# Product-key mixing: the second and third piece of the weight multiplied on GpSimd instead of the vector engine

## The reference, cut to what matters

```python
def _L0_ffn_ref(x, w_q, keys, expert_down, expert_up, norm_w):
    H, DK, K = (8, 128, 8)
    NKEYS = 64                      # 64 * 64 = 4096 experts
    xn = _rmsnorm(x, norm_w)
    q = (xn @ w_q.T).reshape(b, t, H, 2, DK)
    sim1 = jnp.einsum('bthd,hkd->bthk', q[..., 0, :], keys[:, :, 0, :])
    sim2 = jnp.einsum('bthd,hkd->bthk', q[..., 1, :], keys[:, :, 1, :])
    s1, i1 = jax.lax.top_k(sim1, K)
    s2, i2 = jax.lax.top_k(sim2, K)
    all_idx = (i1[..., :, None] * NKEYS + i2[..., None, :]).reshape(b, t, H, K * K)
    all_sc = (s1[..., :, None] + s2[..., None, :]).reshape(b, t, H, K * K)
    fs, pk = jax.lax.top_k(all_sc, K)
    fi = jnp.take_along_axis(all_idx, pk, axis=-1)
    hidden = jax.nn.gelu(jnp.einsum('btd,bthkd->bthk', xn, expert_down[fi]), approximate=False)
    hidden = hidden * jax.nn.relu(fs)
    return jnp.einsum('bthk,bthkd->btd', hidden, expert_up[fi])
```

## Time and profile before

| What | us |
|---|---|
| median of 3 runs | 523.21 |
| lowest, highest | 519.38, 525.88 |
| the profiled execution's own time | 523.5 |
| its span, first to last instruction | 521.7 |
| TensorE busy in the span | 465.3 |
| vector engine busy | 286.6 |
| scalar engine busy | 171.2 |
| GpSimd busy | 4.1 |
| the mixing stage, from its first matmul to its last weighing | 318.9 to 350.0 |

### The profile page before, as it was taken

The page is one execution under the profiler, slowest core; times in us unless marked ns, Lnnn a source line. Parts: engine busy times, 40 slices in busy tenths (PEclk is TensorE's granted clock), DMA queues, the critical chain, the costliest instruction groups (busy, mean ns, idle before and its releaser), DMA issues.

```text
span 521.7 us, 8539 instructions
## 1 busy us (share of the span) xinstructions
PE 465.3 (89%) x3199; PEld 325.7 (62%) x3199; DVE 286.6 (55%) x925; ACT 171.2 (33%) x428; POOL 4.1 (1%) x6
## 2 busy tenths in 40 slices
PE   3888999878999889977769989989979999889997
PEld 2534554443545459874456878878855668767774
DVE  5155777455767644457746997960045444445332
ACT  1154555434555511364731232000013233124110
POOL 0000000000000000000000002000000000000000
PEclk9898999889999999998888999659999999989999
DMA  8300001000002910800004945600048000000000
GB/s 293 105 2 1 1 0 42 1 0 0 0 0 61 363 64 1 322 2 1 1 1 142 336 143 188 136 0 0 1 132 318 1 1 0 1 0 2 0 1 21
DMA packets 21469, 35.02 MB, mean 67 GB/s; under 512 B 1663, under 2 KB 18048, under 8 KB 20864
## 3 DMA queue, kind: packets, MB, share of 16 engines
q1 hardware_dynamic: 21440, 34.64, 20.5%
HBM read 34.37 MB, written 0.26 MB: 66 GB/s over the span
## 4 chain that ended last, share of the span: by engine, by line
PE 73%; DVE 16%; issue 5%; ACT 2%; DMA 1%; DVEq 0%; SPq 0%; POOL 0%; ACTq 0%
PE bank L553 6%; PE bank L538 6%; PE bank L793 6%; PE bank L931 5%; PE bank L527 4%; PE bank L495 4%; PE bank L847 3%; PE bank L492 3%; PE bank L493 3%; PE bank L825 3%; PE bank L826 3%; PE bank L783 2%; PE bank L471 2%; PE bank L945 1%; DMA region_a<-in_Wq 1%
## 5 line engine op out<-in xcount | busy, mean ns | idle before, releaser
L1002 ACT ACTIVATE region_g<-bank,nm_new 128x512 f32<-128x512 f32 x64 | 43.4, 683 | 59.8 <-DVE nm_new L1250 59.8
L538 PEld LDWEIGHTS bank<-ident,region_g 128*128 128x128 f32 x256 | 28.8, 145 | 36.3 <-ACT region_d L1014 24.4
L538 PE MATMUL bank<-ident,region_g 128*128 128x128 f32 x256 | 36.9, 289 | 12.1 <-ACT region_d L1014 7.4
L1245 DVE CUSTOM_DVE_ANT_0 bank<-bank,bias_h 128x512 f32<-128x512 f32 x64 | 43.0, 713 | 4.5 <-issue 4.5
L527 PE MATMUL bank<-region_a,qT 64*128 64x512 f32 x128 | 34.6, 619 | 0.0
L1221 DVE COPY region_a<-bank 128x512 f32<-128x512 f32 x18 | 12.5, 692 | 38.3 <-PE bank L497 38.3
L553 PE MATMUL bank<-region_d,region_a 128*64 128x256 f32 x256 | 32.8, 400 | 0.0
L793 PE MATMUL bank<-region_u,region_g 128*128 128x256 f32 x128 | 29.6, 396 | 1.5 <-issue 1.5
L318 ACT ACTIVATE root<-var 128x2 f32<-128x2 f32 x6 | 1.2, 203 | 87.7 <-DVE var L328 87.7
L783 PE MATMUL bank<-region_a 64*128 64x32 bf16 x768 | 27.3, 249 | 2.4 <-DVE region_a L1499 1.8
L793 PEld LDWEIGHTS bank<-region_u,region_g 128*128 128x128 f32 x128 | 25.5, 200 | 5.3 <-issue 1.6
(11 more groups left out here) (299 smaller groups left out, 833.9 us busy)
## 6 DMA issues: line engine op xcount, KB each, us to landing
region_d<-in_downT SPq DMA_DIRECT2D x2, 2048.0 KB, 10.6
region_u<-in_up SPq DMA_DIRECT2D x2, 2048.0 KB, 11.9
region_a<-in_ctx SPq DMA_DIRECT2D x1, 3072.0 KB, 16.5
region_d<-in_w_q SPq DMA_DIRECT2D x1, 2048.0 KB, 12.3
region_d<-in_ctxT SPq DMA_DIRECT2D x1, 2048.0 KB, 11.5
region_u<-in_wg SPq DMA_DIRECT2D x1, 1728.0 KB, 7.8
region_u<-in_wu SPq DMA_DIRECT2D x1, 1728.0 KB, 11.7
region_a<-in_wd SPq DMA_DIRECT2D x1, 1664.0 KB, 15.9
```

What stands on the lines that cost most here:

```text
L538: mm = nc.tensor.transpose(bank[4 + e][:, k * P:(k + 1) * P], prob[:, u % 2, e, k * P:(k + 1) * P], ident[:, :])
L1002: nc.scalar.activation(prob[:, u % 2, e, :], bank[2 * s + e][:, :], ACT.Exp, scale=-1.0, bias=nm_new[:, p, t, e:e + 1], accum_out=l_blk[:, ...
L1245: ins = nc.vector.tensor_tensor_reduce(bank[2 * s + e][:, :], bank[2 * s + e][:, :], bias_h[:, t, :], -1.0, 3e38, ALU.add, ALU.min, accum_ ...
```

## The change

GpSimd makes the products for the pieces w = 1 and w = 2; the vector engine keeps w = 0. A new semaphore `rest_ready` counts GpSimd's part, and TensorE waits for it beside `hot_ready`. GpSimd's two multiplications of a step wait for that step's `hit_ready`; they stand behind the memset and a wait for its end.

```diff
@@ -290,6 +290,7 @@
+        rest_ready = sem("rest_ready")
@@ -775,6 +776,7 @@
                 for g in range(2):
                     pe.wait_ge(hot_ready, two + (g + 1))
+                    pe.wait_ge(rest_ready, two + (g + 1))
                     pe.wait_ge(hidden_ready, two + (g + 1))
@@ -1495,9 +1497,7 @@
                 nc.vector.tensor_tensor(hit_hi[:, g], iota_h[:, 0:ET], over(1, ET), ALU.is_equal).then_inc(hit_ready, 1)
                 nc.vector.tensor_tensor(hot_lo[:, g], iota_h, over(0, P), ALU.is_equal)
                 dve.wait_ge(hit_ready, n)
-                for w in range(3):
-                    ins = nc.vector.tensor_tensor(hot_hi[:, g, w], hit_hi[:, g], over(2 + w, ET), ALU.mult)
-                ins.then_inc(hot_ready, 1)
+                nc.vector.tensor_tensor(hot_hi[:, g, 0], hit_hi[:, g], over(2, ET), ALU.mult).then_inc(hot_ready, 1)
@@ -1691,6 +1691,20 @@
             pool.wait_ge(down_psum, ET // 2)
             nc.gpsimd.memset(ctxT_b[CD - P:CD - P + 1], 1.0).then_inc(ones4_set, 1)
+            pool.wait_ge(ones4_set, 1)
+
+            def rest_pieces(g, n, at):
+
+                pool.wait_ge(hit_ready, n)
+                for w in (1, 2):
+                    rest = chosen_h[:, 2 + w, bass.ds(at, GS)].unsqueeze(1).to_broadcast([P, ET, GS])
+                    ins = nc.gpsimd.tensor_tensor(hot_hi[:, g, w], hit_hi[:, g], rest, ALU.mult)
+                ins.then_inc(rest_ready, 1)
+
+            with pool.Fori(0, P // GS // 2) as i:
+                two, at = pool.snap(i * 2), pool.snap(i * (2 * GS))
+                rest_pieces(0, two + 1, at)
+                rest_pieces(1, two + 2, at + GS)
```

## The result

| | before | changed |
|---|---|---|
| median of 6 runs, us | 523.33 | 541.82 |
| lowest, highest | 519.38, 525.88 | 539.77, 548.86 |
| the profiled execution's own time | 523.5 | 541.67 |
| its span | 521.7 | 539.9 |

Ratio 1.0389, 95% interval 1.0339 to 1.0439: slower by 17.7 to 23.0 us (the two medians differ by 18.5). The slowest execution of the changed kernel, 548.86 us, showed a lower granted clock than the others, and the ratio leaves it out. The prediction was 534.0 (527 to 542) on a 523.5 base: right in sign, and nearly half of the loss is missing from it. That 541.82 lies just inside the range is luck: the range reached so far only because a multiplication might take 1.7 us, and none takes that by itself. The forecast was +10.5, the ratio says +20, and most of the difference is a term that the prediction did not have.

The account below looks back on a forecast made before the run. TensorE bounds the whole program, the vector engine sets the mixing steps' pace. Later start and GpSimd's chain end step 7 at 359.2 instead of 348.7: 523.5 + 10.5 = 534.0 us, range 527 to 542.

Parts of the forecast that it names:

- The start: Ahead of step 0: TensorE waits for GpSimd's memset and two multiplications, until 324.35 instead of 318.92, costing 5.4 us.
- The loop: Mixing steps: waiting for GpSimd's products makes them 4.52 us each instead of 3.72, with step 7 ending at 359.2.
- The ring: Even and odd steps each form a cycle: chain of 5.6 us plus matmuls of 3.44, 9.05 us per two steps.
- The link that was too dear: End of the loop's chain: after the low one-hot, the vector engine's product, 0.33 us, then GpSimd's two, 2.4 us.
- The signs that I had named: Expected profile: first matmul near 324.3, TensorE idle about 1.1 us a step, GpSimd as releaser, steps about 4.5 us apart.
- Turns, not overlap: In the loop, vector engine and GpSimd instructions reading two SBUF operands alternate, GpSimd behind; chain 5.6 us, chance 0.45.
- rival 1: In the loop, the engines do not hold each other up: chain 4.25 us, +5.6, 529.1 us; chance 0.23.
- The duration of 1.2 us: One GpSimd multiplication in the loop, taken between bounds of 0.45 and 1.7 us, so 2.4 us a step.
- rival 2: GpSimd's multiplication is dear, 1.7 us or more: start 325.35, chain 6.6, +16.2, 539.7 us; chance 0.22.
- rival 3: GpSimd's multiplication is cheap, 0.45 us without turns, TensorE bounds the loop: +1.7, 525.2 us; chance 0.10.
- My ceiling: Most that faster products can win in the mixing steps: 0.28 us in each of eight, 2.2 us, 0.4% of the run.
- The floor of 3.44 us: Time of a mixing step's 96 matmuls on TensorE, below which a step was taken not to fall.

Follow-up runs that it names:

- The two shadow runs: Kernel before, GpSimd's multiplication loaded early, GpSimd also making two unused products a step (534.45 us), or two memsets in their place (521.64 us).
- The version beside the weighing: Changed kernel with only the third piece on GpSimd, run during the vector engine's weighing; tiny multiplication early, memset behind the loop: 518.06 us.
- the control: Kernel before with only the vector engine's loop written out, constants instead of registers: 522.47 us, ratio 0.9988.
- both pieces beside the weighing: Changed kernel with high one-hot ahead of weighing and GpSimd's two products started when matmuls end; tiny multiplication early, memset behind the loop: 523.75 us.
- the run with the memset last: Changed kernel with a tiny GpSimd multiplication issued early and the memset of line 1693 moved behind the loop: 525.14 us, ratio 1.0128.
- the load-alone run: Kernel before plus a tiny GpSimd memset and multiplication behind line 1693's memset, which TensorE awaits ahead of step 0: 535.43 us.
- the last version: Changed kernel, only third piece on GpSimd during the weighing, tiny multiplication early, memset behind the loop, 4 MB of late loads held back: 517.44 us.

## Why the prediction was wrong, point by point

**The start: right in what it counted, and one term missing.** The step that failed is the sum "321.75 + about 0.1 to notice + 2.4 + 0.1 = 324.35", a wait of 5.4 us. With the load out of the way the wait for step 0 is 5.50, so memset and two products were priced well (alone a product lasts 1.14 to 1.17 us: four take 4.52). But between the memset and the first multiplication there were 12.61 us, not 0.1. I took GpSimd's first use of an operation to cost what later ones do. The trace of before could not price it: its only GpSimd instruction besides memsets is the reduction, and the MODIFY_POOL_CONFIG records of its line stand at the very start, at 0.8 us, 228 us ahead of it. But they are there, and I did not ask what they were for. The Trainium skill (GPSIMD Engine Reference, Instruction dispatch) says that the first call to freshly loaded GpSimd code pays about 6 us, 5.95 measured, with no instruction in the profile that shows it. The runs agree in kind and give more: 6.8 to 7.6 us with quiet DMA engines, 10.78 and 12.61 with 4 MB of transfers running. A rival "the code has to be loaded first" belonged into the prediction.

**The loop: right in mechanism, a little too dear.** From step 0 to the last matmul I had 359.2 - 324.35 = 34.85, it was 33.59, against 29.76 before: +3.8 where I counted +5.1. The ring is there: in the changed kernel step 2 ends at 345.33 and step 4 starts at 350.67, 5.34 us for my 5.6; steps come in alternate gaps (4.00, 4.72, 4.06), two of them 8.71 to 8.78 for my 9.05. The link that was too dear is the last: from the low one-hot's end (348.16, where the next instruction starts) to GpSimd's last result (350.56) three products, the vector engine's one and GpSimd's two, took 2.40 us, where I had added up 0.33 + 2.4. The record of GpSimd's first product starts 0.36 us after the low one-hot has started, but it is longer than alone, 1.89 us against 1.15, and ends at 349.27, one product's length behind the one-hot: it waited for it. The vector engine's product then waits behind GpSimd's first, 1.40 us instead of 0.42, which is not the order that I had assumed.

**The signs that I had named.** The first matmul came at 333.26, not near 324.3. The idle time before each later step alternates between 0.6 and 1.3 us, 0.9 in the mean for my 1.1, and the steps are 4.3 us apart in the mean for my 4.5. GpSimd was to stand there as the releaser; the profile names none, but the times above do. "Stretched vector instructions" came true for the product alone; the one-hots kept 0.42 and 1.22 us.

**Turns, not overlap: right.** It was my choice, with no row of before behind it. The two shadow runs show it (3.01 against 1.09 us, and 1.09 when GpSimd only writes), and rival 1 falls. For the second half the rows of before had more than I used: not only the high one-hot but also the low one (1.22) and the three products (1.09) ran under the memset with their usual lengths.

**The duration of 1.2 us: right, with some luck.** It was the middle between bounds of 0.45 and 1.7 that had little behind them. Measured: 1.15 alone, 1.34 in the median over the whole loop, where some wait for their turn. Rivals 2 and 3 fall. The figure of the Trainium skill (GPSIMD Engine Reference, Performance versus the Vector engine), which is for an addition of float32 values, had given an estimate of 1.12 us, close to the 1.15. Two sums of the rivals were wrong without touching the forecast: by its own steps rival 2 ends at 364.2 (539.0 us), not 364.9, and rival 3's chain is 2.75 us, not 2.35.

**The sum.** By stretch: start 5.6 (5.4 expected), loop 3.8 (5.1 expected), load 12.2 (not expected), together 21.6 for 10.5. Without the missing term the forecast would have been a little too high.

**What removing vector work could win: right, but not in this order.** The version beside the weighing took 1.55 us off the stretch, and 3.0 with the pause in step 1 gone as well. My ceiling, "8 x 0.28 = 2.2 us", is met by the 2.3 that are left without the pause, but by two errors that cancel. The floor of 3.44 us for a step is too high, since a lone burst contains the whole last matmul: two steps in one piece take 6.63 us, 3.3 each. And not all eight steps of before waited: the first three ran without a wait, but for the pause. The change itself gave its saving back, since each GpSimd product blocks the vector engine's for about a microsecond (3.01 - 1.09 = 1.92 us for two).

## What to carry to other kernels

The first multiplication on GpSimd carried a cost that no duration shows, in all likelihood a code load (7 us here, over 12 beside bulk transfers): issue a tiny one early, where nobody waits, before judging an offload. When work moves to GpSimd, add up all instructions of both engines that read two SBUF operands as if one engine ran them, and place GpSimd's beside vector instructions that read PSUM. And look at where the helper engine's queue stands: here a memset that TensorE waits for only 66 us later (in the kernel before at 387.8, line 815) stood ahead of the critical product.

## What the runs showed that I had not expected

- The gap ahead of the first multiplication depends on the bulk transfers: 12.6 us with 4 MB in flight and 7.3 without, in otherwise the same kernel. The page's queue rows do not show why: 18 packets of queue q8 and 11 of q14 in the kernel before and in the changed one.
- TensorE stopped behind the 161st of the small mixing matmuls while the late transfers ran: 0.65 us in the kernel before, 0.53 in the control, 0.46 with both pieces beside the weighing, 0.87 to 3.56 in other runs. It did not where the transfers were held back, nor where it had stood for more than 12 us ahead of the stage, and hardly in the run with the memset last.
- From GpSimd's last write to TensorE's first matmul took 0.38 us in the load-alone run and 0.10 to 0.11 in the changed kernel's loop, but the vector engine started 0.03 us after the reduction's end.
- In the last version TensorE's granted clock stayed at 1.00 (2.4 GHz) through the stage, where in the later steps of before it was 0.50 (1.2 GHz):

```profile
330.00:334.00 4.00, 4.00 (x123) 3.90 (x121) 1.00 0.00 0
```

  The columns are the stretch, its width, TensorE's matmuls and weight loads of the mixing line, the clock, the DMA share and GB/s. The matmuls were no shorter for it: 248 ns on average there and 249 in the kernel before, as the prediction assumed.
